# Two-layer transformer with mixtures of experts: GpSimd's gather and scatter programs unrolled, and layer 0's result rows written to a place of their own instead of being added up in DRAM

## The chip, the cores and the metric

One NeuronCore of one Trainium2 chip runs the whole program in one launch. The metric is the device time of an execution in microseconds (us).

## The reference

Two layers over x of 2 batches x 512 tokens x 256 channels (T = 1024 tokens in all), all in float32. Each layer is an adaLN block: a modulated layer norm, causal attention with 16 heads, a gated residual, a second modulated norm, and a mixture of experts.

```
x = x + ga * attention(layernorm(x) * (1 + ca) + sa)
h = layernorm(x) * (1 + cb) + sb
x = x + gb * mixture(h)
layer 0: 8 experts, top 2:  y = sum over the 2 chosen e of gate[e] * (W2[e] silu(W1[e] h + b1[e]) + b2[e])
layer 1: 16 experts, top 4: h + sum over the 4 chosen e of gate[e] * (W2[e] act(W1[e] rms(h) + b1[e]) + b2[e])
```

What matters here is the sum over a token's chosen experts. In layer 0 each token has exactly two result rows of 256 floats, in layer 1 four.

## The kernel before, in words

**The mixture.** Tokens are sorted by expert into tiles of 128 places. Every tile belongs to one expert: layer 0 has 23 tiles (SLOTS_T[0]), layer 1 has 47. Places that no token takes are filled with pad rows T to T + 127, one for each partition (lane). DVE works out a place for each token and choice, PE turns that into a table by matmuls with zeros and ones (L1520, into bank 4), and DVE makes two tables of it: `weight` (gate of the row at place p of tile i) and `token` (its row number in DRAM, L1171 to L1174). `te` holds each tile's expert (L1175 to L1178).

**One tile** then runs through the engines. POOL gathers its 128 rows from DRAM (`xs`, which the trace calls token_rows) into one of four buffers `xt` with an indirect DMA (L612). PE transposes it (L1534), multiplies by W1 (L1549 bias, L1552), transposes (L1561) and multiplies by W2 (L1570 bias, L1573), each for another tile of a pipeline four steps deep. ACT applies the gate weight and writes the result tile to one of four buffers `yt` (L820, semaphore y_sb). POOL adds its 128 rows into DRAM with an indirect DMA that adds (L619), into one of two tables of sums, by the parity of the tile. ACT may write `yt` of tile i only when the add of tile i - 4 has landed.

**POOL's program** is the order in question. POOL is a queue that runs in order. In step s it waits for its index copy, for the result of tile s - 7 (LAG = 7), for the landing of the add of tile s - 9, and for PE's transposes of tile s - 3; then it copies the indices of step s + 1 out of the table `token` into a small tile `indices` (`pick`, L603), gathers tile s, and adds tile s - 7. So two adds are in flight at most. Eleven steps are written out, the middle of each layer is a loop of four steps a turn, and the last seven steps, which have only an add, are written out too. A layer has SLOTS_T + 7 steps.

**After the last tile** SP (in order as well) waits for the adds of tiles of one parity, issues four loads of that table (256 KB each, L508), waits for the other parity and issues four more. For each quarter of the tokens, DVE (POOL for the last quarter) adds the two tables, multiplies by the gate and adds to x (L1257 to L1261; POOL L660 to L667). In layer 0 the norm and attention of layer 1 follow behind it; in layer 1 the output's stores (L516). Meanwhile PE and DVE work out layer 1's modulation (PE after the last y_sb of layer 0, L1280 and L1299; DVE up to L893).

**Zeroing.** The four tables of sums (two a layer, 1152 KB each) are zeroed by SP's DMAs (L468) during layer 0's attention, behind the loads of the expert weights (L464) and the small transfers of maxima (L442).

Of the kernel before, what the change touches and what calls it, by code (L numbers as in the profile page):

```python
# [10 lines left out]
P = 128  # L11
D = 256
# [3 lines left out]
T = B * S  # L16
NT = T // P
# [26 lines left out]
TOPK = [2, 4]  # L44
# [10 lines left out]
UNROLL = 4  # L55
STEADY = 7
LAG = 7
PICKS_BEFORE = [0, SLOTS_T[0] + LAG]
POOL_STEADY = 11
# [7 lines left out]
def build_kernel(nc, dram, out):  # L67
    with ExitStack() as ctx:
        def sb(name, shape, dt=F32):
            return ctx.enter_context(nc.sbuf_tensor(name, shape, dt))  # L70

        def sem(name):
            return ctx.enter_context(nc.semaphore(name))
# [153 lines left out]


        xs = [nc.dram_tensor(f"token_rows{l}", [T + P, D], F32, kind="Internal") for l in range(2)]
        acc = [[nc.dram_tensor(f"sums{l}_{a}", [T + P, D], F32, kind="Internal") for a in range(2)] for l in range(2)]  # L230


        ld_const = sem("ld_const")
# [66 lines left out]
        token_picked = sem("token_picked")  # L300
        placed_ps = sem("placed_ps")
        acc_loaded = sems("acc_loaded", 4)
        h_rows = sem("h_rows")
# [118 lines left out]
        def _(sp):  # L422
# [20 lines left out]
                        qr[SROWS + r:SROWS + r + 1, (g // 2) % 2, hl:hl + HG, :],  # L443
                        mT[r * 16:(r + 1) * 16, g % 2, :]).then_inc(m_rows[l][g % 2], 16)

            ZERO_AT = [0, 1, 5, 6]

            for l in range(2):
                spread_unit(sp, nc.sync, l, 0, (0, 1), spread[0])
# [7 lines left out]
                for g in range(NG):  # L457
                    if g in (3, 5):

                        u = (g + 1) // 2  # L460
                        spread_unit(sp, nc.sync, l, u, (1,), spread[u])
                    send_maxima(l, g)
                    piece = slice(g * WROW[l], (g + 1) * WROW[l])
                    nc.sync.dma_start(big[:, piece], dram[f"moe{l}"][:, piece]).then_inc(ld_w_lo[l], 16)  # L464
                    if l == 0 and g in ZERO_AT:

                        z = ZERO_AT.index(g)
                        nc.sync.dma_start(acc[z // 2][z % 2][:, :].rearrange("(t p) c -> p t c", p=P),  # L468
                                          zeros[:, :].unsqueeze(1).broadcast_to([P, NT + 1, D])).then_inc(zeroed, 16)
# [31 lines left out]


                sp.wait_ge(y_ps[l], n)
                for a in ((n - 2) % 2, (n - 1) % 2):
                    for r in (a, a + 2):
                        sp.wait_ge(y_summed[r], TILES_BEFORE[l + 1][r])
                    for m in (3, 0, 1, 2):
                        nc.sync.dma_start(acc_in[:, a, 2 * m:2 * m + 2, :],  # L508
                                          acc[l][a][2 * m * P:(2 * m + 2) * P, :].rearrange("(t p) c -> p t c", p=P)
                                          ).then_inc(acc_loaded[m], 16)  # L510
            for m in (0, 3, 1, 2):
                if m < NT // 2 - 1:
                    sp.wait_ge(x_new[1], m + 1)
# [8 lines left out]
        def _(pool):  # L522
# [10 lines left out]
            for l in range(2):  # L533
# [58 lines left out]
                def pick(ii, off):  # L592

                    i, r, _ = tile_at(ii, off)
                    n = SLOTS_T[l]
                    gathers, adds = takes_part(ii, off)
                    if gathers and adds:
                        src, dst = token[:, bass.ds(i - LAG, LAG + 1)][:, ::LAG], indices[:, r, :]
                    elif gathers:
                        src, dst = token[:, i:i + 1], indices[:, r, 1:2]  # L600
                    else:
                        src, dst = token[:, i - LAG:i - LAG + 1], indices[:, r, 0:1]
                    nc.gpsimd.tensor_copy(dst, src).then_inc(token_picked, 1)  # L603

                def takes_part(ii, off):

                    known, n = isinstance(ii, int), SLOTS_T[l]
                    return not known or off < n, not known or 0 <= off - LAG < n

                def gather(off):  # L610
                    r = off % 4
                    nc.gpsimd.indirect_dma_start(  # L612
                        out=xt[:, r, :], out_offset=None, in_=xs[l][:, :],
                        in_offset=bass.IndirectOffsetOnAxis(ap=indices[:, r, 1:2], axis=0)).then_inc(xt_loaded[r], 16)

                def add_rows(off):
                    r = off % 4
                    place_r = (off + LAG) % 4
                    nc.gpsimd.indirect_dma_start(  # L619
                        out=acc[l][off % 2][:, :],  # L620
                        out_offset=bass.IndirectOffsetOnAxis(ap=indices[:, place_r, 0:1], axis=0),
                        in_=yt[:, r, :], in_offset=None, compute_op=ALU.add).then_inc(y_summed[r], 16)

                def pool_step(ii, off):
                    gathers, adds = takes_part(ii, off)
                    i, _, _ = tile_at(ii, off)

                    pool.wait_ge(token_picked, PICKS_BEFORE[l] + i + 1)
                    if adds:

                        pool.wait_ge(y_sb[l], i - LAG + 1)
                        if not (isinstance(i, int) and i < LAG + 2):
                            _, r2, rnd2 = tile_at(ii, off - LAG - 2)
                            pool.wait_ge(y_summed[r2], TILES_BEFORE[l][r2] + 16 * rnd2 + 16)
                    if gathers and not (isinstance(i, int) and i < 3):

                        pool.wait_ge(xT_ps[l], i - 2)
                    if not isinstance(ii, int) or off + 1 < SLOTS_T[l] + LAG:
                        pick(ii, off + 1)
                    if gathers:  # L640
                        gather(off)
                    if adds:
                        add_rows(off - LAG)

                pool.wait_ge(zeroed, 16 * 6)
                pool.wait_ge(rows_stored[l], 16 * B)
                pool.wait_ge(tokens_ready, l + 1)
                pick(0, 0)
                for s in range(POOL_STEADY):
                    pool_step(0, s)  # L650
                with pool.Fori(0, (SLOTS_T[l] - POOL_STEADY) // UNROLL) as ii:
                    for q in range(UNROLL):
                        pool_step(ii, POOL_STEADY + q)
                for s in range(SLOTS_T[l], SLOTS_T[l] + LAG):
                    pool_step(0, s)

                m = NT // 2 - 1
                rng = slice(2 * m, 2 * m + 2)
# [186 lines left out]
        def _(dve):  # L845
# [74 lines left out]
            for l in range(2):  # L920
# [157 lines left out]
                E, K = EXPERTS[l], TOPK[l]  # L1078
                if l == 0:
                    dve.wait_ge(ld_small, 64)  # L1080
                oh = onehot[:, 0:NT * K * E].rearrange("p (t k e) -> p t k e", t=NT, k=K)
                ch = chosen[:, 0:NT * E].rearrange("p (t e) -> p t e", t=NT)
                for b in range(B):
# [49 lines left out]
                for b in range(B):  # L1133
# [16 lines left out]
                    for t in range(b * TB, (b + 1) * TB):  # L1150
                        c = slice(t * K, (t + 1) * K)
                        nc.vector.tensor_tensor(
                            in_tile(l, t), first[:, c].unsqueeze(2).broadcast_to([P, K, MT[l]]),
                            iota_t128[:, 0:MT[l]].unsqueeze(1).broadcast_to([P, K, MT[l]]),
                            ALU.is_equal).then_inc(tile_of[l], 1)
                        nc.vector.tensor_tensor(
                            at_p[:, c, :], place[:, c].unsqueeze(2).broadcast_to([P, K, P]),
                            iota_p.unsqueeze(1).broadcast_to([P, K, P]), ALU.is_equal)
                        dve.wait_ge(tile_of[l], t + 1)
                        nc.vector.tensor_scalar(weighed_tile(l)[:, c, 0, :], in_tile(l, t), left[:, t:t + 1], None,  # L1160
                                                ALU.mult).then_inc(place_of[l], 1)
# [7 lines left out]
                sums = ps[4][:, 0:2 * MT[l]].rearrange("p (a c) -> p a c", a=2)  # L1169
                w = slice(0, MT[l])  # L1170
                count(nc.vector.tensor_copy(weight[:, w], sums[:, 1, :]))  # L1171
                link(nc.vector.tensor_scalar(token_f[:, w], sums[:, 0, :], 0.0, lane[:, 0:1], ALU.is_equal, ALU.mult))
                link(nc.vector.tensor_tensor(token_f[:, w], token_f[:, w], sums[:, 0, :], ALU.subtract))
                nc.vector.tensor_scalar(token[:, w], token_f[:, w], float(T), None, ALU.add).then_inc(tokens_ready, 1)  # L1174
# [523 lines left out]
```

## Time and profile before

| | |
|---|---|
| median of 3 runs | 691.54 us (691.23 to 694.9) |
| span of the profiled execution, first to last instruction | 693.0 us |
| layer 0's mixture, first gather to last add landed | 203.8 to 287.6 us |
| layer 1's mixture, first gather to last add landed | 502.6 to 676.6 us |
| busy share over the span: PE, DVE, ACT, POOL | 77%, 54%, 35%, 39% |
| indirect DMAs on POOL | 70 gathers, 70 adds |
| mean granted TensorE clock | 0.881 of full speed |

The profile covers one execution; its span is the time that it shows for itself, and it lies 1.5 us above the median. An indirect DMA has two durations: how long the instruction holds POOL, and the time from its start to the landing of its data, which is when its semaphore is complete. "issue" is time in which the engine waited for nothing that the profile shows.

### The profile page before, as it was taken

How to read it: one execution, taken by the hardware profiler on the slowest of the kernel's cores; microseconds unless marked ns; L12 is line 12 of the kernel's file. 1: busy time of each engine (PE TensorE's matmuls, PEld its weight loads, DVE VectorE, ACT ScalarE, POOL GpSimd, SP SyncE). 2: the span in 40 equal slices, each digit the busy share in tenths (PEclk: the TensorE clock that was granted, in tenths of full speed). 3: DMA queues.
4: the chain of work that ended last, by engine and by line, in shares of the span. 5: the costliest groups of instructions: out<-in, count | busy, mean ns of one | idle time of the engine just before them, and what ended most of it. 6: DMA issues, size and time to landing. Idle time of an engine off the chain costs nothing.

```text
span 693.0 us, 10488 instructions
## 1 busy us (share of the span) xinstructions
PE 531.5 (77%) x3140; PEld 343.4 (50%) x3141; DVE 371.5 (54%) x854; ACT 245.4 (35%) x542; POOL 269.0 (39%) x285
## 2 busy tenths in 40 slices
PE   4679977987649777637897879863679999999960
PEld 3344544545547665315454445543636666666630
DVE  4855756545663222288386636566934444544424
ACT  1225534554132222003264335521424444444420
POOL 2300103001026888430001150046048888888852
PEclk9898989899658999959799989995679999999995
DMA  7097466634103545707828272173013444444445
GB/s 269 2 131 145 122 100 110 127 106 178 61 16 67 83 80 70 156 2 96 99 81 136 62 124 94 50 318 111 0 54 70 77 79 73 79 79 83 71 52 180
DMA packets 44499, 67.41 MB, mean 97 GB/s; under 512 B 6417, under 2 KB 37857, under 8 KB 44209
## 3 DMA queue, kind: packets, MB, share of 16 engines
q1 hardware_dynamic: 29872, 45.45, 27.4%
q0 software_dynamic: 14592, 21.51, 19.4%
q8 instruction: 21, 0.34, 0.2%
q14 instruction: 14, 0.11, 0.1%
HBM read 36.83 MB, written 17.30 MB: 78 GB/s over the span
## 4 chain that ended last, share of the span: by engine, by line
PE 51%; DMA 15%; DVE 13%; ACT 6%; POOL 5%; issue 5%; SPq 4%; POOLq 0%; DVEq 0%; ACTq 0%
PE bank L1552 13%; PE bank L1573 6%; DMA big<-parts 5%; DMA sums<-ptm,indices 5%; PE bank L1399 5%; PE bank L1442 4%; PE bank L1418 4%; ACT ptm L757 3%; SPq L409 3%; PE bank L1372 3%; DVE mx L1022 3%; PE bank L1520 3%; DMA big<-mT 2%; PE bank L1534 2%; POOL ptm L612 2%
## 5 line engine op out<-in xcount | busy, mean ns | idle before, releaser
L1022 DVE TENSOR_REDUCE mx<-bank 128x4 f32<-128x512 f32 (+2 forms) x96 | 99.2, 1042 | 76.1 <-PE bank L1402 75.4
L619 POOL DMA_INDIRECT sums<-ptm,indices x70 | 113.2, 1617 | 22.9 <-issue 21.2
L1552 PE MATMUL bank<-big,ptm 128*128 x280 | 111.7, 522 | 0.0
L757 ACT ACTIVATE ptm<-bank 128x512 f32<-128x512 f32 x160 | 90.3, 596 | 53.3 <-PE bank L1421 51.0
L1418 PE MATMUL bank<-big 98*128 98x128 bf16 (+3 forms) x256 | 68.8, 326 | 22.8 <-DMA big<-mT 14.2
L1399 PE MATMUL bank<-big 96*128 96x128 bf16 (+3 forms) x256 | 67.3, 329 | 15.8 <-DMA big<-parts 11.6
L409 POOL DMA_DIRECT2D big<-parts x24 | 13.0, 553 | 166.1 <-PE bank L1421 166.1
L612 POOL DMA_INDIRECT ptm<-token_rows,indices x70 | 70.3, 1004 | 17.0 <-issue 12.9
L1573 PE MATMUL bank<-big,ptm 128*128 (+1 forms) x280 | 72.1, 379 | 0.0
L603 POOL COPY indices<-token 128x2 uint32 (+2 forms) x84 | 43.4, 516 | 57.1 <-DVE token L1174 42.6
L1214 DVE TENSOR_SCALAR tok<-bank 128x256 f32<-128x256 f32 x47 | 19.9, 424 | 84.9 <-PE bank L1552 84.9
L1552 PEld LDWEIGHTS bank<-big,ptm 128*128 128x128 f32 x280 | 51.0, 197 | 26.6 <-issue 23.6
L531 POOL TENSOR_TENSOR rstd<-vareps,neghalf 128x4 f32<-128x4 f32 x8 | 8.6, 1072 | 122.6 <-DVE vareps L906 122.6
L1418 PEld LDWEIGHTS bank<-big 98*128 98x128 bf16 x256 | 26.6, 104 | 54.6 <-ACT ptm L757 25.2
L1402 PE MATMUL bank<-constb 128*128 128x128 bf16 x256 | 52.7, 234 | 0.0
L1421 PE MATMUL bank<-constb 128*128 128x128 bf16 x256 | 50.9, 233 | 0.0
L804 ACT ACTIVATE ctxden<-tok 128x256 f32<-128x256 f32 x47 | 19.6, 417 | 86.2 <-DVE tok L1214 86.2
L1573 PEld LDWEIGHTS bank<-big,ptm 128*128 128x128 f32 (+1 forms) x280 | 47.5, 190 | 4.8
L1399 PEld LDWEIGHTS bank<-big 96*128 96x128 bf16 x256 | 26.6, 104 | 36.1 <-issue 25.1
L820 ACT ACTIVATE ptm<-bank,weight 128x256 f32<-128x256 f32 x70 | 33.1, 473 | 27.9 <-PE bank L1573 25.5
L1442 PE MATMUL bank<-ptm,big 128*32 128x128 f32 (+3 forms) x512 | 39.4, 447 | 1.4 <-ACT ptm L757 1.4
L1534 PE MATMUL bank<-consts,ptm 128*128 128x128 f32 x140 | 28.6, 288 | 11.2 <-DMA ptm<-token_rows,indices 11.2
(174 smaller groups left out, 872.3 us busy)
## 6 DMA issues: line engine op xcount, KB each, us to landing
big<-parts SPq DMA_DIRECT2D x72, 128.0 KB, 7.7
big<-in_moe_dram SPq DMA_DIRECT2D x8, 768.0 KB, 4.3
big<-in_moe_dram SPq DMA_DIRECT2D x1, 6144.0 KB, 19.6
sums<-zeros SPq DMA_DIRECT2D x4, 1152.0 KB, 6.4
ptm<-sums SPq DMA_DIRECT2D x16, 256.0 KB, 4.6
big<-in_moe_dram SPq DMA_DIRECT2D x8, 432.0 KB, 4.0
big<-parts POOLq DMA_DIRECT2D x24, 128.0 KB, 5.1
wqkv<-in_wqkv_dram SPq DMA_DIRECT2D x2, 768.0 KB, 6.8
```

What stands on the lines that cost most here:

```text
L603: nc.gpsimd.tensor_copy(dst, src).then_inc(token_picked, 1)
L612: nc.gpsimd.indirect_dma_start(out=xt[:, r, :], out_offset=None, in_=xs[l][:, :], in_offset=bass.IndirectOffsetOnAxis(ap=indices[:, r, 1:2 ...
L619: nc.gpsimd.indirect_dma_start(out=acc[l][off % 2][:, :], out_offset=bass.IndirectOffsetOnAxis(ap=indices[:, place_r, 0:1], axis=0), in_=y ...
L757: nc.scalar.activation(dst, src, ACT.Exp).then_inc(b_exp[l], 1)
L1022: nc.vector.tensor_reduce(mx[:, g % 2, :].rearrange("p (j i) -> p j i", j=HG)[:, j0:j0 + n, i], a_view(c), AX.X, ALU.max).then_inc(a_max[l ...
L1399: nc.tensor.matmul(dst[:, j, :], qr[0:SROWS, u % 2, hl, i * P:(i + 1) * P], kr[0:SROWS, u % 2, hl, 0:w], start=True, stop=False)
L1402: last = nc.tensor.matmul(dst[:, j, w - P:w], ident_b, causal_b, start=False, stop=True)
L1418: nc.tensor.matmul(ps[4 + c % 2][:, col:col + S - k * P], kr[0:MROWS, u % 2, hl, k * P:(k + 1) * P], qr[0:MROWS, u % 2, hl, k * P:S], star ...
L1421: last = nc.tensor.matmul(ps[4 + c % 2][:, col:col + P], causal_b, ident_b, start=False, stop=True)
L1442: last = nc.tensor.matmul(ps[6][32 * j:32 * j + 32, k * P:S], vaug[:, b * TB + k, hg * HG + j, :], pt[:, g % 2, j, PK[k]:PK[k] + S - k * P ...
L1552: last = nc.tensor.matmul(dst, xtT[:, off % 2, k, :], moe_w1(l, k, e), start=False, stop=(k == KD - 1))
L1573: last = nc.tensor.matmul(dst, hidT[0:HK[l], off % 2, k, :], moe_w2(l, k, e), start=False, stop=(k == 1))
```

## The change

- `pick` and the tile `indices` are gone. Gathers and scatters read their indices straight from a column of a table. Both layers' steps are written out: no loop, 30 steps in layer 0 and 54 in layer 1.
- Each gather now waits only for PE's transposes of tile i - 4. The wait for a result stands directly before the scatter.
- Layer 0: the table `pairs` has two halves of T + 128 rows, one for each choice. A second table of indices, `dest`, names the half, and `put_rows` writes the rows without addition. It waits for the landing of the scatter before it (i - 1), where the add waited for i - 2. SP waits for all scatters before it loads anything.
- Layer 1: `add_rows` adds as before, with the wait for i - 2, into the two tables that were zeroed for it. Two of the four zeroings are gone.
- DVE carries the choice through the table of places: the token's number has 2048 added for choice 1 (`leftk`), which is taken off again afterwards.

```diff
-        indices = sb("indices", [P, 4, 2], U32)
+        dest = sb("dest", [P, MT[0]], U32)
+        upper = sb("upper", [P, MT[0]])
+        leftk = sb("leftk", [P, NT * TOPK[0]])
...
+        pairs = nc.dram_tensor("pairs", [2 * ROWS, D], F32, kind="Internal")
+        sums = [nc.dram_tensor(f"sums{a}", [ROWS, D], F32, kind="Internal") for a in range(2)]
...
-            ZERO_AT = [0, 1, 5, 6]
+            ZERO_AT = [0, 1]
...
                 sp.wait_ge(y_ps[l], n)
+                if l == 0:
+                    for r in range(4):
+                        sp.wait_ge(y_summed[r], TILES_BEFORE[1][r])
                 for a in ((n - 2) % 2, (n - 1) % 2):
-                    for r in (a, a + 2):
-                        sp.wait_ge(y_summed[r], TILES_BEFORE[l + 1][r])
+                    if l == 1:
+                        for r in (a, a + 2):
+                            sp.wait_ge(y_summed[r], TILES_BEFORE[2][r])
...
+                def gather(i):
+                    if i >= 4:
+                        pool.wait_ge(xT_ps[l], i - 3)
                     nc.gpsimd.indirect_dma_start(
+                        out=xt[:, i % 4, :], out_offset=None, in_=xs[l][:, :],
+                        in_offset=bass.IndirectOffsetOnAxis(ap=token[:, i:i + 1], axis=0)).then_inc(xt_loaded[i % 4], 16)
+                def put_rows(i):
+                    pool.wait_ge(y_sb[0], i + 1)
+                    if i >= 1:
+                        pool.wait_ge(y_summed[(i - 1) % 4], 16 * ((i - 1) // 4) + 16)
                     nc.gpsimd.indirect_dma_start(
+                        out=pairs[:, :], out_offset=bass.IndirectOffsetOnAxis(ap=dest[:, i:i + 1], axis=0),
+                        in_=yt[:, i % 4, :], in_offset=None).then_inc(y_summed[i % 4], 16)
+                def add_rows(i):
+                    pool.wait_ge(y_sb[1], i + 1)
+                    if i >= 2:
+                        pool.wait_ge(y_summed[(i - 2) % 4], TILES_BEFORE[1][(i - 2) % 4] + 16 * ((i - 2) // 4) + 16)
...
+                for s in range(SLOTS_T[l] + LAG):
+                    if s < SLOTS_T[l]:
+                        gather(s)
+                    if s >= LAG:
+                        if l == 0:
+                            put_rows(s - LAG)
+                        else:
+                            add_rows(s - LAG)
...
+                if l == 0:
+                    link(nc.vector.tensor_scalar(upper[:, :], placed[:, 0, :], SECOND - 0.5, float(SECOND), ALU.is_gt, ALU.mult))
+                    link(nc.vector.tensor_tensor(upper[:, :], placed[:, 0, :], upper[:, :], ALU.subtract))
+                    link(nc.vector.tensor_scalar(token_f[:, w], upper[:, :], 0.0, lane[:, 0:1], ALU.is_equal, ALU.mult))
+                    link(nc.vector.tensor_tensor(token_f[:, w], token_f[:, w], upper[:, :], ALU.subtract))
+                    count(nc.vector.tensor_scalar(token[:, w], token_f[:, w], float(T), None, ALU.add))
+                    link(nc.vector.tensor_scalar(upper[:, :], placed[:, 0, :], SECOND - 0.5, float(ROWS), ALU.is_gt, ALU.mult))
+                    nc.vector.scalar_tensor_tensor(dest[:, :], token_f[:, w], float(T), upper[:, :], ALU.add,
+                                                   ALU.add).then_inc(tokens_ready, 1)
```

In `link` DVE waits for its own instruction before the next; in `count` it doesn't.

## Rows read from the trace of the kernel before

**Rows 1.** The page: chain that ended last by engine, and the group of picks.

```profile
PE 51%; DMA 15%; DVE 13%; ACT 6%; POOL 5%; issue 5%; SPq 4%; POOLq 0%; DVEq 0%; ACTq 0%
...
L603 POOL COPY indices<-token 128x2 uint32 (+2 forms) x84 | 43.4, 516 | 57.1 <-DVE token L1174 42.6
```

**Rows 2.** Windows: us; busy (x) of PE, PEld, DVE, ACT, POOL; PEclk; DMA share; GB/s.

```profile
225.55:268.07 42.52, 31.93 (x187) 25.39 (x185) 11.41 (x27) 10.75 (x27) 36.43 (x40) 1.00 0.50 81
...
560.00:600.00 40.00, 40.00 (x169) 25.52 (x168) 19.13 (x48) 17.29 (x48) 32.98 (x37) 1.00 0.47 75
```

**Rows 3.** Timeline of POOL, layer 0, one steady step (start us, us, instruction).

```profile
241.91 1.59 POOL L619 DMA_INDIRECT sums<-ptm,indices  x1 [0.30 <-issue]
242.93 0.77 POOL L603 COPY indices<-token 128x2 uint32 x1
243.87 1.00 POOL L612 DMA_INDIRECT ptm<-token_rows,indices  x1 [0.16 <-POOL indices L603]
245.18 1.60 POOL L619 DMA_INDIRECT sums<-ptm,indices  x1 [0.30 <-issue]
```

**Rows 4.** Timeline of ACT, layer 0: the first two result tiles.

```profile
216.41 0.47 ACT L820 ACTIVATE ptm<-bank,weight 128x256 f32<-128x256 f32 x1 [0.88 <-PE bank L1573]
...
218.55 0.47 ACT L820 ACTIVATE ptm<-bank,weight 128x256 f32<-128x256 f32 x1 [0.88 <-PE bank L1573]
```

**Rows 5.** Timeline of POOL, layer 0: adds of tiles 0, 15 and 22.

```profile
218.94 1.64 POOL L619 DMA_INDIRECT sums<-ptm,indices  x1 [0.30 <-PE bank L1534]
...
268.07 1.59 POOL L619 DMA_INDIRECT sums<-ptm,indices  x1 [0.30 <-issue]
...
283.77 1.55 POOL L619 DMA_INDIRECT sums<-ptm,indices  x1 [0.41 <-issue]
```

**Rows 6.** Chain in order of time, the end of layer 0's mixture (start us, us, what).

```profile
283.77 3.88 DMA sums<-ptm,indices
287.71 0.37 SPq L508
288.12 5.92 DMA ptm<-sums
```

**Rows 7.** Chain in order of time, layer 1's last adds, tiles 44 and 46.

```profile
666.27 0.48 ACT ptm L820
...
667.52 3.91 DMA sums<-ptm,indices
...
671.50 0.69 issue
672.19 4.44 DMA sums<-ptm,indices
```

**Rows 8.** Source view of L619, the adds (durations ns min/median/max, then landings).

```profile
L619 POOL DMA_INDIRECT sums<-ptm,indices x70: 1552/1597/1829, 218.9 to 672.2; - x70
...
DMA to landing us min/median/max: 3.6/3.8/4.4
```

**Rows 9.** Source view of L612, the gathers.

```profile
L612 POOL DMA_INDIRECT ptm<-token_rows,indices x70: 967/1007/1117, 203.8 to 652.1; - x70
...
DMA to landing us min/median/max: 2.6/2.8/4.6
```

**Rows 10.** Timelines of DVE and POOL: layer 0's token table and first gather.

```profile
202.41 0.18 DVE L1173 TENSOR_TENSOR token_f<-token_f,bank 128x24 f32<-128x24 f32 x1
202.62 0.18 DVE L1174 TENSOR_SCALAR token<-token_f 128x24 uint32<-128x24 f32 x1
...
203.78 1.12 POOL L612 DMA_INDIRECT ptm<-token_rows,indices  x1 [0.38 <-issue]
```

**Rows 11.** Timeline of SP: the eight loads of layer 0's sums.

```profile
285.58 4.08 SPq L508 DMA_DIRECT2D ptm<-sums  x8
```

**Rows 12.** Timeline of DVE: the end of layer 1's modulation.

```profile
290.12 0.41 DVE L893 TENSOR_SCALAR modbc<-bank 128x256 f32<-128x256 f32 x1
```

**Rows 13.** Waits between 118 and 150 us, where the dropped zeroings run.

```profile
PE bank L1418 <- DMA big<-mT: 2.9, 1, 2.9
```

More of the change, by code:

```diff
@@ L229, in build_kernel, with summand @@
         xs = [nc.dram_tensor(f"token_rows{l}", [T + P, D], F32, kind="Internal") for l in range(2)]
-        acc = [[nc.dram_tensor(f"sums{l}_{a}", [T + P, D], F32, kind="Internal") for a in range(2)] for l in range(2)]
+        pairs = nc.dram_tensor("pairs", [2 * ROWS, D], F32, kind="Internal")
+        sums = [nc.dram_tensor(f"sums{a}", [ROWS, D], F32, kind="Internal") for a in range(2)]
+        def summand(l, a, lo, hi):
+            src = pairs[a * ROWS + lo:a * ROWS + hi, :] if l == 0 else sums[a][lo:hi, :]
+            return src.rearrange("(t p) c -> p t c", p=P)
         ld_const = sem("ld_const")
@@ L590, in _ @@
                         nc.gpsimd.tensor_tensor(x[:, rng, :], x[:, rng, :], tok[:, rng, :], ALU.add).then_inc(h_added, 1)
[L592 to L611, printed above, removed]
-                    nc.gpsimd.indirect_dma_start(
-                        out=xt[:, r, :], out_offset=None, in_=xs[l][:, :],
-                        in_offset=bass.IndirectOffsetOnAxis(ap=indices[:, r, 1:2], axis=0)).then_inc(xt_loaded[r], 16)
@@ L616, in add_rows @@
-                def add_rows(off):
-                    r = off % 4
-                    place_r = (off + LAG) % 4
-                    nc.gpsimd.indirect_dma_start(
[L620 to L643, printed above, removed]
@@ new lines, in add_rows @@
+                def add_rows(i):
+                    pool.wait_ge(y_sb[1], i + 1)
+                    if i >= 2:
+                        pool.wait_ge(y_summed[(i - 2) % 4], TILES_BEFORE[1][(i - 2) % 4] + 16 * ((i - 2) // 4) + 16)
+                    nc.gpsimd.indirect_dma_start(
+                        out=sums[i % 2][:, :], out_offset=bass.IndirectOffsetOnAxis(ap=token[:, i:i + 1], axis=0),
+                        in_=yt[:, i % 4, :], in_offset=None, compute_op=ALU.add).then_inc(y_summed[i % 4], 16)
@@ L646, in _ @@
+                pool.wait_ge(zeroed, 16 * 4)
                 pool.wait_ge(rows_stored[l], 16 * B)
                 pool.wait_ge(tokens_ready, l + 1)
[L648 to L655, printed above, removed]
+                for s in range(SLOTS_T[l] + LAG):
[6 more added lines that the diff above has]
+                            add_rows(s - LAG)
@@ L1080, in _ @@
                     dve.wait_ge(ld_small, 64)
+                    dve.wait_ge(ld_const, 16)
+                    by_k = leftk[:, :].rearrange("p (t k) -> p t k", k=K)
+                    count(nc.vector.tensor_copy(by_k[:, :, 0], left))
+                    count(nc.vector.tensor_scalar(by_k[:, :, 1], left, float(SECOND), None, ALU.add))
                 oh = onehot[:, 0:NT * K * E].rearrange("p (t k e) -> p t k e", t=NT, k=K)
@@ L1159, in _ @@
                         dve.wait_ge(tile_of[l], t + 1)
-                        nc.vector.tensor_scalar(weighed_tile(l)[:, c, 0, :], in_tile(l, t), left[:, t:t + 1], None,
-                                                ALU.mult).then_inc(place_of[l], 1)
+                        if l == 0:
+                            nc.vector.tensor_tensor(weighed_tile(0)[:, c, 0, :], in_tile(0, t),
+                                                    leftk[:, c].unsqueeze(2).broadcast_to([P, K, MT[0]]),
+                                                    ALU.mult).then_inc(place_of[0], 1)
+                        else:
+                            nc.vector.tensor_scalar(weighed_tile(1)[:, c, 0, :], in_tile(1, t), left[:, t:t + 1], None,
+                                                    ALU.mult).then_inc(place_of[1], 1)
                 pk = picked[0:1, 0:n * E].rearrange("p (t e) -> p t e", t=n)
@@ L1168, in _ @@
                 dve.wait_ge(placed_ps, l + 1)
-                sums = ps[4][:, 0:2 * MT[l]].rearrange("p (a c) -> p a c", a=2)
+                placed = ps[4][:, 0:2 * MT[l]].rearrange("p (a c) -> p a c", a=2)
                 w = slice(0, MT[l])
[L1171 to L1174, printed above, removed]
+                count(nc.vector.tensor_copy(weight[:, w], placed[:, 1, :]))
+                if l == 0:
+                    link(nc.vector.tensor_scalar(upper[:, :], placed[:, 0, :], SECOND - 0.5, float(SECOND), ALU.is_gt, ALU.mult))
[6 more added lines that the diff above has]
+                                                   ALU.add).then_inc(tokens_ready, 1)
+                else:
+                    link(nc.vector.tensor_scalar(token_f[:, w], placed[:, 0, :], 0.0, lane[:, 0:1], ALU.is_equal, ALU.mult))
+                    link(nc.vector.tensor_tensor(token_f[:, w], token_f[:, w], placed[:, 0, :], ALU.subtract))
+                    nc.vector.tensor_scalar(token[:, w], token_f[:, w], float(T), None, ALU.add).then_inc(tokens_ready, 1)
                 link(nc.vector.tensor_reduce(tef[:, 0:n], pk, AX.X, ALU.add))
```

11 lines of the change are left out of this document (4 added, 7 removed).

## The prediction, made before the change was run

> **What bounds the kernel now.** I read the page first. Its chain is half PE, and POOL has only 5% of it, though the picks alone keep POOL busy for 43.4 us [rows 1]. So what a shorter program on POOL is worth must be read stage by stage, and the table of windows does that. In layer 1's mixture PE is busy 40.00 of 40 us and POOL 32.98: PE sets the pace. In layer 0's mixture PE is busy 31.93 of 42.52 us and POOL 36.43, the rest of POOL's time being short gaps of issue [rows 2]. POOL sets the pace there. Its timeline shows why: from one add to the next are 3.27 us (241.91 to 245.18), made of the add's 1.60, what is left of the pick, a gather of 1.00 and gaps of 0.16 and 0.30 [rows 3]. ACT's first two result tiles came 2.14 us apart, before any add was issued [rows 4]; that is how fast the other engines can go.
>
> At layer 0's end the gathers are over and each add waits for the landing of the one two before it. Tile 15's add starts at 268.07 and tile 22's at 283.77, so 2.24 us each, with two in flight [rows 5]. The last lands 3.88 us after its start, at 287.65. Then come SP's loads and DVE [rows 6].
>
> **What the change does, part by part.**
>
> *The wait of the plain scatter.* This is the term that decides. Put i waits until put i - 1 has landed, not i - 2. So each of layer 0's 22 steps between puts costs at least the landing time L, plus the restart of a waiting POOL. The restart stands at the end of layer 1: tile 44's add lands at 671.43, tile 46's, which waited for it with no pick between, starts at 672.19, so 0.76 us [rows 7]. The same step without any wait would be gather, put and two gaps: 1.00 + 1.00 + 0.60 = 2.60 us if a put holds POOL as long as a gather. The gather between two puts lies inside the wait for the landing and costs nothing; if landings became that short, it would set the pace of 2.60.
>
> *L itself* is in no row, for no plain scatter runs before. An add holds POOL 1.60 us and lands 3.8 us after its start [rows 8]. A gather, also 128 rows of 1 KB without addition, holds it 1.00 and lands after 2.8, at least 2.6 [rows 9]. I bound L by 2.6 and 3.8 and take 2.8: the put has the gather's bytes, rows and indices and lacks the addition, which needs the old row read before the new one is written. The step is then 2.8 + 0.76 = 3.56 us, longer than the 3.27 it replaces and much longer than the 2.24 of the tail.
>
> The Trainium skill (DMA: Bandwidth & Descriptors, Anatomy of one DMA — SWDGE path) says otherwise of the direction: most of the fixed cost of a small transfer is the receipt of the last write, and DRAM (HBM) is the slowest target. [...] What a slow write would do is the first rival.
>
> *Head of layer 0.* DVE's table chain has four more dependent instructions ahead of the token signal. One costs 0.21 us (202.41 to 202.62) [rows 10]: +0.8. Between the end of the token table (202.80) and the first gather (203.78) lie 0.98 us with two picks; a restart without a pick is 0.76: -0.2. Together +0.6 for the first gather, +0.5 for the first results, since later picks are gone too. The first y ended at 216.88 [rows 4] and now ends at 217.4. Before, the first add stood behind gather 7, which itself waited for that y; now gather 7 goes ahead of the wait, and put 0 starts at 217.4 + 0.76 = 218.15 (before 218.94 [rows 5]). The broadcast multiply of DVE in place of the scalar one has as many elements, and the two `leftk` instructions run while DVE waits for PE's gate logits: nothing; uncovered, they would cost 0.4.
>
> *Sum to the last landing.* Put 22 starts at 218.15 + 22 x 3.56 = 296.5 and lands at 299.3. Before it was 287.65: **+11.6 us**. PE and ACT wait for free `yt` buffers meanwhile, at no further cost, because their own pace is 2.14.
>
> *SP's loads.* Before, the four loads of the first parity were issued from 285.58, two us ahead of the last landing [rows 11], and the load that DVE waited for was issued 0.47 us after that landing and took 5.92 [rows 6]. Now all eight come after it, the deciding one is the sixth, and one issue takes 0.5 us: it leaves at about +2.5. **+2.0 us.** Layer 1's modulation, done at 290.53 before the loads landed at 294.04 [rows 6, 12], hangs on the last y, which needs put 18 landed (about 285 us) and so ends near 297, with the loads landing near 307: hidden. If put 18 were later still, both move together.
>
> *Layer 1.* First gathers earlier by the picks and the shorter restart: -0.3. Steady tiles: PE's, unchanged. Tail: tile 44's add started 0.77 us after its y was done, pick included [rows 7], and the restart without one is 0.76: nothing. Code written out in place of the loop: POOL has no loop cost in its steady step [rows 3] beyond the gaps; nothing, and if instruction fetches stalled it, layer 1's cover is POOL's idle 7 of 40 us [rows 2] and layer 0's is the wait.
>
> *Two zeroings less.* In their stretch the only wait for a transfer is PE's 2.9 us for the maxima, which come from SP's queue ahead of the zeroing [rows 13]: nothing, at most -0.5.
>
> **Sum**: 11.6 + 2.0 - 0.3 = +13.3 us. Against the profiled span that is 706.3; that execution lies 1.5 above the median, so the forecast is 691.5 + 13.3 = **704.8 us**. Each 0.1 us of L moves it by 23 x 0.1 = 2.3. With L from 2.6 to 3.0 it is 700.2 to 709.4, the forecast's own range.
>
> **The rivals.**
>
> 1. *Writes to DRAM are confirmed more slowly than reads from it.* After its 1.60 on POOL the add still took 2.2 us, the gather 1.8 [rows 8, 9]. If that 0.4 belongs to the write and not to the addition, L = 1.0 + 2.2 = 3.2: put 22 lands at 218.15 + 22 x 3.96 + 3.2 = 308.5, +20.8, in all +22.5: **714 us**. For it: the add's row; against: the addition also reads the old rows. This is also the direction of the Trainium skill's rule.
> 2. *The long hold of POOL is the scatter's, not the addition's.* Then a put holds 1.60, L is 3.4 (gather's 1.8 behind it) to 3.8: **718.6 to 727.8 us**. For it: every scatter in the trace holds 1.55 or more; against: the one difference known between the two forms is the addition's extra read.
> 3. *The other side: plain rows land so soon that the wait is over before the gather between is issued.* Then POOL's own 2.60 sets the pace and L is at most 2.3: put 22 lands at 218.15 + 57.2 + 2.3 = 277.7, -10.0; with the loads -8.3: **683.3 us**. It decides from 22 steps + L = 67.8 us on; with the full restart that is L = 2.2. Against: the quickest of 70 gathers took 2.6. For: a restart might overlap the gather's own issue, which with L = 2.6 and the steady step's 0.30 gap in place of 0.76 gives 22 x 2.9 + 2.6 = 66.4, 1.4 less, so about 690.
> 4. *Nothing to see*: the slower steps and the saved picks cancel. That takes L of 2.2 to 2.4 or such an overlap: **688 to 695 us**.
>
> **How the numbers follow.** Forecast 0.47, rival 1 0.20, rival 2 0.18, rival 3 0.09, rival 4 0.06. The range reaches from 697, where a restart shorter by a few tenths would put the forecast, to 721, which holds rival 1 and the lower half of rival 2; outside lie rivals 3 and 4 and rival 2's end, some 0.2. A measurement of this kernel tells about 0.5% or 3.5 us from no change. Faster by more: 0.08 (rival 3); within: 0.07; slower: 0.85.
>
> **What the changed profile would show.** The step: POOL's timeline with puts about 3.5 us apart and idle time before each, released by the DMA of the put before; PE waiting for ACT or for gathers, its busy share in that stretch down from 0.75 to about 0.7. L: the put's landing in its source view, near 2.8, and its duration near 1.0. The tail: no speeding up after the last gather. The loads: eight in one run after the last landing. Layer 1: the same 40 of 40 us on PE and the last adds at the same distance from the last y. I am wrong if puts stand 2.6 to 3.2 us apart, if they land in under 2.4, or if layer 1's tiles change their pace.

## The result and the profile after

The changed kernel is slower: 698.68 us median of 5 runs (697.45 to 702.78) against 692.52 us, a ratio of 1.0098 (95% interval 1.0063 to 1.0134). That is inside the range on record (697 to 721), near its lower end, and on the side it named, but about half of the +13.3 us that was forecast, and below the forecast's own range (700.2 to 709.4). Ratios are of executions in the fast state; one of the twelve of after_again below took 1765 us and is left out of its ratio.

The profiled execution spans 700.9 us. POOL's timeline in layer 0, two steady steps and the tail (start us, us, instruction, idle before it), answers to [rows 3] and [rows 5]:

```profile
225.64 0.99 POOL L615 DMA_INDIRECT pairs<-ptm,dest  x1 [0.97 <-ACT ptm L803]
226.93 0.97 POOL L606 DMA_INDIRECT ptm<-token_rows,token  x1 [0.30 <-issue]
228.83 0.99 POOL L615 DMA_INDIRECT pairs<-ptm,dest  x1 [0.93 <-DMA pairs<-ptm,dest]
...
267.31 0.99 POOL L615 DMA_INDIRECT pairs<-ptm,dest  x1 [0.94 <-DMA pairs<-ptm,dest]
270.50 0.99 POOL L615 DMA_INDIRECT pairs<-ptm,dest  x1 [2.20 <-DMA pairs<-ptm,dest]
...
289.48 0.97 POOL L615 DMA_INDIRECT pairs<-ptm,dest  x1 [2.20 <-DMA pairs<-ptm,dest]
```

A put holds POOL 0.99 us, then comes the gather, which ends at 227.90. The put before has landed 2.43 us after its start, at 228.07, and the next put starts 0.76 us later: of POOL's 0.93 us of idle time 0.17 are the rest of the landing and 0.76 the restart. From put to put are 3.19 us, and that does not change when the gathers end (267.31 to 270.50): only the idle time grows. The first row names ACT as what ended the wait, since a put waits for its result too. But that result had been ready since 223.14, 2.5 us before. From put 1 on, all results were ready 1.4 to 9.7 us ahead of their puts, and each put started 0.7 to 0.8 us after the landing of the one before. Before the change a step was 3.27 us [rows 3], but 2.24 in the tail [rows 5].

The source views of the puts (L615) and gathers (L606), against [rows 8, 9]:

```profile
L615 POOL DMA_INDIRECT pairs<-ptm,dest x23: 969/987/999, 219.2 to 289.5; - x23
...
DMA to landing us min/median/max: 2.4/2.4/2.5
```

```profile
L606 POOL DMA_INDIRECT ptm<-token_rows,token x70: 940/992/1102, 205.8 to 657.7; - x70
...
DMA to landing us min/median/max: 2.6/2.8/3.3
```

The chain at layer 0's end, against [rows 6]. Two of the steps between puts and the end:

```profile
286.31 2.43 DMA pairs<-ptm,dest
...
288.77 0.70 issue
289.48 2.42 DMA pairs<-ptm,dest
...
294.50 5.47 DMA ptm<-pairs
```

The step is 2.43 for the landing and 0.74 for the restart. The load that DVE waits for is the sixth, issued at 294.50, 2.6 us after the last landing. The last put lands at 291.90; DVE's first combination starts at 299.99, 8.09 us later, where it was 6.42 before (294.07 - 287.65).

Layer 1 is as it was: in the windows view PE is busy 40.00 of 40 us from 560 to 600, while POOL's share fell with the picks (32.98 before [rows 2]).

```profile
560.00:600.00 40.00, 40.00 (x169) 25.37 (x167) 19.24 (x48) 17.53 (x48) 30.79 (x25) 1.00 0.49 79
```

From its first gather to the start of its last add layer 1 takes 168.60 us (511.55 to 680.15), before 169.55 (502.64 to 672.19).

**Where the 6 us are.** From layer 0's first gather to its last landing 86.07 us (205.83 to 291.90) against 83.87: +2.2. From there to DVE +1.7. DVE's longer chain for the tables +0.6 (from its copy of the weights to the first gather 2.38 us against 1.74). Layer 1's mixture -0.95. That makes +3.6.

The two profiled spans differ by more, 7.9 us (700.9 against 693.0). The other 4.4 us lie in stretches whose work is the same in both kernels: 1.4 ahead of layer 0's tables, and 3.0 between DVE's first combination and layer 1's first gather (211.56 us against 208.57). The first are TensorE's clock. In the windows view the first fence is before and has PE alone (us, busy, PEclk, DMA share, GB/s); the second is after and has PE, PEld, DVE, ACT and POOL ahead of PEclk:

```profile
166.00:170.00 4.00, 2.47 (x33) 1.00 0.78 332
```

```profile
166.00:170.00 4.00, 3.30 (x29) 1.16 (x22) 0.21 (x1) 0.60 (x1) 0.73 (x1) 0.62 0.77 326
```

The granted clock was 0.62 of full speed on the mean of these 4 us, that is, partly at the lower of its two levels (1.2 GHz), although the work is the same in both kernels. In both, PE had been idle for 0.69 us, waiting for ACT's exponentials, just before the group of 32 matmuls at 165 us; that group took 4.05 us after and 2.36 before. This fall is in 4 of the 14 profiled executions of this document, so it comes and goes. The 3.0 us come and go as well: in a second execution of the changed kernel that stretch took 207.66 us.

### The profile page after: what moved, and what is told of

Its sections match the earlier page's. It is cut to its first block, busy times and chain, and to the rows that moved or that the text cites. A ratio compares the mean times of both kernels' runs of the same rounds, so it can differ in the third digit from the quotient of the medians.

```text
span 700.9 us, 10178 instructions
## 1 busy us (share of the span) xinstructions
PE 536.8 (77%) x3140; PEld 346.7 (49%) x3141; DVE 372.6 (53%) x860; ACT 245.7 (35%) x542; POOL 235.0 (34%) x201
## 3 DMA queue, kind: packets, MB, share of 16 engines
q0 software_dynamic: 12384, 21.51, 16.4%
## 4 chain that ended last, share of the span: by engine, by line
PE 53%; DMA 17%; DVE 13%; ACT 6%; issue 5%; SPq 4%; POOL 1%; POOLq 0%; DVEq 0%; ACTq 0%
PE bank L1555 13%; PE bank L1576 7%; DMA pairs<-ptm,dest 6%; DMA big<-parts 5%; PE bank L1402 5%; PE bank L1445 5%; PE bank L1421 4%; ACT ptm L740 3%; SPq L416 3%; PE bank L1375 3%; DVE mx L1005 2%; PE bank L1537 2%; DMA big<-mT 2%; PE bank L1552 2%; PE bank L1564 2%
## 5 line engine op out<-in xcount | busy, mean ns | idle before, releaser
L606 POOL DMA_INDIRECT ptm<-token_rows,token x70 | 68.8, 983 | 70.0 <-DVE dest L1172 24.9
L624 POOL DMA_INDIRECT sums<-ptm,token x47 | 74.5, 1584 | 31.9 <-ACT ptm L803 30.2
L1445 PE MATMUL bank<-ptm,big 128*32 128x128 f32 (+3 forms) x512 | 42.9, 479 | 1.4 <-ACT ptm L740 1.4
L1316 PE MATMUL bank<-consts,tok 128*128 128x128 f32 x80 | 14.3, 337 | 30.9 <-DVE tok L898 26.5
```

The lines of the kernel that those rows point to most:

```text
L606: nc.gpsimd.indirect_dma_start(out=xt[:, i % 4, :], out_offset=None, in_=xs[l][:, :], in_offset=bass.IndirectOffsetOnAxis(ap=token[:, i:i ...
L624: nc.gpsimd.indirect_dma_start(out=sums[i % 2][:, :], out_offset=bass.IndirectOffsetOnAxis(ap=token[:, i:i + 1], axis=0), in_=yt[:, i % 4, ...
L1445: last = nc.tensor.matmul(ps[6][32 * j:32 * j + 32, k * P:S], vaug[:, b * TB + k, hg * HG + j, :], pt[:, g % 2, j, PK[k]:PK[k] + S - k * P ...
```

## The experiments

### The program written out, nothing else

Layer 0 adds as before the change, with the wait for the add two before; only `pick`, `indices` and the loops are gone.

```diff
-                pick(0, 0)
-                for s in range(POOL_STEADY):
-                    pool_step(0, s)
...
+                for s in range(SLOTS_T[l] + LAG):
+                    if s < SLOTS_T[l]:
+                        gather(s)
+                    if s >= LAG:
+                        add_rows(s - LAG)
```

> The kernel before with POOL's program written out and indices read from the token table; layer 0 still adds, with the wait for the add two before. Theory (the loss is the serial wait for each put's landing, and writing the program out helps a little): layer 0's steady step is 1.60 + 0.30 + 1.00 + 0.30 = 3.20 us instead of 3.27, the first add starts 1 to 2 us earlier, the tail keeps its pairs of about 4.6 us, layer 1 keeps PE's pace: 2 to 3 us faster than before, about 690. Rival (writing the program out is itself what costs, by instruction fetches or because gathers run further ahead): slower than before by several us, about 697.

Measured: 688.77 us, ratio to before 0.9917 (0.9885 to 0.995). POOL's timeline, the first add and two steady ones:

```profile
217.32 1.63 POOL L605 DMA_INDIRECT sums<-ptm,token  x1 [1.58 <-ACT ptm L781]
...
242.87 1.59 POOL L605 DMA_INDIRECT sums<-ptm,token  x1 [0.30 <-ACT ptm L781]
244.77 0.99 POOL L596 DMA_INDIRECT ptm<-token_rows,token  x1 [0.30 <-issue]
246.06 1.59 POOL L605 DMA_INDIRECT sums<-ptm,token  x1 [0.30 <-issue]
```

The step is the 3.19 us expected. The first add comes 13.04 us after the first gather at 204.28 (before 15.16), and from first gather to last landing (284.29) are 80.0 us, before 83.9. So this half of the change gains 0.8% alone, more than my 2 to 3 us; the end of the interval nearest to no change is 3.5 us. The rival, that unrolling costs, is out.

### The same with the old waits

Every step waits first for all that it waited for before, and then gathers and adds.

```diff
+                    if s >= LAG:
+                        pool.wait_ge(y_sb[l], s - LAG + 1)
+                    if s >= LAG + 2:
+                        pool.wait_ge(y_summed[(s - LAG - 2) % 4], TILES_BEFORE[l][(s - LAG - 2) % 4] + 16 * ((s - LAG - 2) // 4) + 16)
+                    if 3 <= s < SLOTS_T[l]:
+                        pool.wait_ge(xT_ps[l], s - 2)
```

> As unroll_only, but each step first waits for everything that the step waited for before (the result, the add two before, the transposes of tile s - 3), and only then gathers and adds. Unroll_only took 3.9 us off the stretch from layer 0's first gather to its last landing (80.0 against 83.9), 2.1 of it before the first add. Theory (a gather that no longer stands behind the wait for a result lets the first add start sooner): first gather to first add goes back from 13.0 to about 15 us, the steady step stays at 3.19, the stretch is about 82.1. Rival (it was the missing picks): the first add stays at 13.0 to 13.5 and the stretch at 80.

One execution, 692.21 us. First gather to first add: 14.43 us (204.60 to 219.03), between 13.04 and 15.16 and nearer the theory. The last add starts 77.8 us after the first gather (at 282.41), in the kernel without the old waits 76.5, before 80.0. One execution of each is thin, for the same POOL program brings its first put 12.77 to 13.69 us after the first gather in four executions (below). What separates the causes better is the distance from ACT's first result to the first add: 0.28 us without the old waits, 1.72 with them, 2.06 before. So 1.4 us of the earlier start come from gathers that no longer stand behind a result; the rest, 0.4 us ahead of that result and 0.3 behind it, went with the picks and the loop.

### Puts that add

The changed kernel with the addition put back into its puts, and nothing else in POOL's program but its wait for two more zeroings, since both halves of the table have to be zeroed first.

```diff
-                        in_=yt[:, i % 4, :], in_offset=None).then_inc(y_summed[i % 4], 16)
+                        in_=yt[:, i % 4, :], in_offset=None, compute_op=ALU.add).then_inc(y_summed[i % 4], 16)
```

> The changed kernel, but layer 0's put adds to its row again (both halves of the table zeroed first); the wait for the put just before stays. Theory: a step is landing plus restart, so 3.8 + 0.76 = 4.56 us instead of 3.19; 22 steps and the last landing cost 31 us more than the changed kernel: about 730. Rival (POOL's own work sets the step, the wait is hidden): 1.60 + 1.00 + 0.60 = 3.20, no change against the changed kernel: about 699.

Measured: 730.25 us, ratio 1.0514 (1.0462 to 1.0566). The chain in layer 0:

```profile
273.15 3.78 DMA pairs<-ptm,dest
...
276.98 0.73 issue
277.70 3.77 DMA pairs<-ptm,dest
```

3.78 for the landing and 0.77 for the restart make the step of 4.55 us. The same wait therefore costs what the landing costs, and the time went where landing plus restart said (730) and not to POOL's own work (699). The puts hold POOL 1.586 us here and 0.987 in the changed kernel, and land after 3.8 and 2.4: both differences belong to the addition.

### Pads apart

In the changed kernel every tile's pads go to the same 128 rows, and successive tiles may both write them; therefore the wait for the put just before. Nothing reads those rows: SP's loads take rows 0 to T - 1 of each half. Here four successive tiles have pad rows of their own, and that wait is loosened to the put two before, or dropped.

```diff
+            for r, off in enumerate((0, ROWS, 2 * ROWS - T, 2 * ROWS + P - T)):
+                nc.gpsimd.memset(padoff[:, r:r + 1], float(off))
...
+                    padadd = token_f[:, MT[0]:2 * MT[0]]
+                    count(nc.vector.scalar_tensor_tensor(padadd.rearrange("p (a b) -> p a b", b=4),
+                                                         placed[:, 0, :].rearrange("p (a b) -> p a b", b=4), 0.0,
+                                                         padoff[:, :].unsqueeze(1).broadcast_to([P, MT[0] // 4, 4]),
+                                                         ALU.is_equal, ALU.mult))
...
+                    link(nc.vector.tensor_tensor(upper[:, :], upper[:, :], padadd, ALU.add))
...
-                    if i >= 1:
-                        pool.wait_ge(y_summed[(i - 1) % 4], 16 * ((i - 1) // 4) + 16)
```

> The changed kernel, with the pad rows of four successive tiles sent to four places of their own (two more DVE instructions on the way to the token signal), so that a put need only wait for the landing of the put two before. Theory: layer 0's step falls to POOL's own 1.00 + 0.30 + 1.00 + 0.30 = 2.60 us, and after the last gather the puts follow the results at 1.6 to 2.2 us: the last put lands about 20 us earlier, 678 to 682 us. Rival (the loss is in the eight loads that now wait for the last put, and in layer 1): at most 2 us off the changed kernel, 697 to 699.

> As pads_apart_wait2, with no wait for a landing at all on POOL; only ACT's wait for the buffer of four tiles before is left. Theory: with two in flight the wait is over already, so the same time as with it within 1 us, 678 to 682. A second theory, that landings limit the rate even with two in flight, gives 2 us or more less than pads_apart_wait2. The rival of the loads gives 697 to 699.

Measured: 681.26 us with the wait for i - 2 (ratio 0.9813, 0.9773 to 0.9852) and 681.44 us without (0.9805, 0.9773 to 0.9838). POOL's timeline without the wait:

```profile
240.34 0.99 POOL L616 DMA_INDIRECT pairs<-ptm,dest  x1 [0.30 <-issue]
241.64 0.97 POOL L609 DMA_INDIRECT ptm<-token_rows,token  x1 [0.31 <-PE bank L1544]
242.91 0.99 POOL L616 DMA_INDIRECT pairs<-ptm,dest  x1 [0.30 <-issue]
...
270.27 0.96 POOL L616 DMA_INDIRECT pairs<-ptm,dest  x1 [0.62 <-ACT ptm L804]
```

The step is 2.57 us, POOL's own work, and the last put starts 65.5 us after the first gather at 204.81, in the changed kernel 83.65. Taking the wait off turns the change from 1.0% slower into 1.9% faster than before, although the edit adds two instructions to DVE's chain. That settles the cause: the wait for the put just before, and not the unrolling, the scatter or layer 1. That the two forms are equal also says that two puts in flight are enough, and it rules out the second theory, that landings limit the rate. No run drops the wait while the pads stay together.

Not all 18 us reach DVE's first combination: it starts 14.26 us after the start of the last put, in the changed kernel 10.51. Two lines of DVE's timeline of the same run show what is late next, layer 1's modulation (L877), which holds DVE until 284.4 while POOL already had its loads at 280.76:

```profile
283.96 0.41 DVE L877 TENSOR_SCALAR modbc<-bank 128x256 f32<-128x256 f32 x1
284.53 0.85 DVE L1267 TENSOR_TENSOR ptm<-ptm 128x512 f32<-128x512 f32 x1 [0.16 <-DVE modbc L877]
```

### Loads in pairs

The changed kernel, whose eight loads now all follow the last put, with both halves of a quarter one behind the other.

```diff
+                if l == 0:
+                    for m in (3, 0, 1, 2):
+                        for a in range(2):
+                            nc.sync.dma_start(acc_in[:, a, 2 * m:2 * m + 2, :],
+                                              summand(0, a, 2 * m * P, (2 * m + 2) * P)).then_inc(acc_loaded[m], 16)
```

> The changed kernel, with layer 0's eight loads in the order that DVE uses them: both halves of a quarter behind each other. In the changed kernel 8.1 us lie between the last landing and DVE's first combination, before the change 6.4. Theory (the wait is SP's issue of six loads at 0.5 us and then the transfer): the deciding load becomes the fourth, about 7.1 us. Rival (the transfer's bandwidth alone sets it): 8.1, since POOL's quarter goes first either way and the same bytes are under way. In all at most 1 us off the changed kernel.

> The changed kernel once more, unaltered, on the same chip as loads_paired_timed. Its first profile lost 1.5 us to a fall of TensorE's granted clock near 166 us that the profile of before does not have, and more such in layer 1's attention. Theory (such falls come and go from run to run): the median stays at 1 per cent over before, about 699; the last landing comes 86.1 us after the first gather, as in the first profile. Rival (the falls belong to the changed kernel, for instance through the two zeroings less): the fall near 166 us is there again.

> The kernel of loads_paired, timed. In its one look DVE's first combination came 7.0 us after the last landing instead of 8.1, and the first combination took 2.7 us instead of 4.5, because POOL's own was further ahead. Theory (both gains are real and lie on the way): 3 us under the changed kernel, about 696. Rival (only the order of issue counts, the rest of the 4 us by which that one execution was quicker was the clock): 1 us under it, about 698.

Measured: 694.74 us in one profiled execution; timed in twelve, 695.85 us (ratio to before 1.0024, 0.9997 to 1.0052), beside 698.69 us of the changed kernel on the same chip (1.0093, 1.0059 to 1.0128). In the profiled execution the last put lands at 289.84 and DVE starts at 296.84, so 7.0 us instead of 8.1: the order of the loads counts, and the rival, that only the bytes do, is out. DVE's timeline there, and that of the changed kernel:

```profile
296.84 1.17 DVE L1264 TENSOR_TENSOR ptm<-ptm 128x512 f32<-128x512 f32 x1 [5.29 <-DMA ptm<-pairs]
298.05 0.69 DVE L1266 TENSOR_TENSOR ptm<-ptm,modbc 128x512 f32<-128x512 f32 x1
```

```profile
299.99 1.17 DVE L1260 TENSOR_TENSOR ptm<-ptm 128x512 f32<-128x512 f32 x1 [6.54 <-DMA ptm<-pairs]
301.19 1.64 DVE L1262 TENSOR_TENSOR ptm<-ptm,modbc 128x512 f32<-128x512 f32 x1
```

The same multiplication takes DVE 1.64 us while POOL runs its own over another quarter, and 0.69 us after POOL is done. POOL's own takes 1.59 us beside DVE's and 1.26 alone. The pair order starts POOL's quarter earlier and so gives back 1.1 us of waiting and 1.9 of slowed work (first combination 2.66 us instead of 4.54). These 3 us fit the timed medians, which are 2.8 apart; by the ratios it is 0.7% or 4.8 us. The changed kernel with this order alone can't be told from the kernel before.

The second execution of the unaltered changed kernel had no fall of the clock near 166 us: PEclk 1.00 in that window.

```profile
166.00:170.00 4.00, 2.48 (x35) 1.00 0.63 264
```

From first gather to last landing it took 86.4 us (203.67 to 290.11), as the first profile's 86.1.

### The best kernel, and what binds behind the wait

Pads apart without the wait, loads in pairs, and the signal to POOL as soon as `token` is there.

> pads_apart_no_wait, the loads in pairs, and the token signal sent to POOL as soon as the token table is there, with the second index table after it. In pads_apart_no_wait DVE is busy with layer 1's modulation until 284.4, 3.6 us after the loads were there for POOL, so the paired loads bring nothing here; the earlier token signal starts layer 0 about 1.2 us sooner and the modulation moves with it. Theory (after the wait is gone the modulation sets layer 0's end): 680 us, 1 us under pads_apart_no_wait. Rival (the loads set it): 2 us or more under it.

> As best, with DVE's work on the rows of layer 1's modulation moved behind the first combination and norm of layer 0's end. Theory (in best this work, waiting for PE's 10 us of modulation matmuls, holds DVE back while the loads have landed): the first combination starts 3 to 4 us earlier, about 677 us. Rival (PE's modulation matmuls hold the next projection back anyway, so DVE's order is worth nothing): as best.

Measured: best 677.95 us (0.9769, 0.9724 to 0.9813), best_order 681.39 us (0.9825, 0.979 to 0.9861). Best is 2.5 us under pads_apart_no_wait by the ratios, nearer the rival's 2 us than the theory's 1, though the two intervals overlap. What the theory said of the order is so: DVE's first combination follows its last instruction on the modulation directly.

```profile
284.42 0.69 DVE L1274 TENSOR_TENSOR ptm<-ptm 128x512 f32<-128x512 f32 x1 [0.16 <-DVE modbc L884]
```

It starts 12.39 us after the start of the last put, where it was 14.26. The earlier token signal brings the first gather 0.6 us closer to DVE's tables (2.07 against 2.68 us behind the copy of the weights), half of the 1.2 expected. No gain is shown further on: the first put comes 13.95 us after the first gather, in pads_apart_no_wait 12.39, and one and the same kernel differs by 0.8 us there (loads_paired 13.55, loads_paired_timed 12.77).

In best_order DVE's first combination did start 4.1 us sooner, and the time did not follow; that theory fell. The rival's time, as best, can't be excluded, for the intervals overlap; its reason is not what the trace shows, as ACT's first query projection waits for DVE and not for TensorE (the row below). Two more runs are best again and a kernel that differs from best by these lines:

```diff
+                    if l == 1 and n == 1:
+                        modulation_rows(1, 0)
...
-                    modulation_rows(1, 0)
```

> The kernel of best once more, beside best_late_rows on the same chip: 2.3 per cent under before, 676 to 679.

> As best, with DVE's work on the rows of layer 1's modulation still later than in best_order: behind both norms and the first two splits of layer 1's projections. In best_order the first combination came 4.1 us earlier than in best, but the second batch's norm stood behind the moved work and the start of layer 1's query projections (ACT at 300.8 against 300.5) did not move. Theory (what binds there is the second norm, so work moved behind it frees both): ACT's first query projection at about 297 and the time 3 us under best. Rival (TensorE's modulation and projections bind, or the moved work now delays the splits by its own 4 us): as best or slower.

Measured: 679.02 us (0.9773, 0.9742 to 0.9803) and 676.45 us (0.9747, 0.9717 to 0.9777). ACT's first query projection of layer 1 in best_order and in best_late_rows:

```profile
300.78 0.69 ACT L710 ACTIVATE tok<-bank,qkb 128x512 f32<-128x512 f32 x1 [7.84 <-DVE qkb L915]
```

```profile
296.36 0.69 ACT L710 ACTIVATE tok<-bank,qkb 128x512 f32<-128x512 f32 x1 [4.22 <-DVE qkb L915]
```

It waits for DVE's L915, which stands behind the second batch's norm. Moving the modulation behind the first norm only shifted it ahead of the second. Moved behind both, it starts 25.75 us after the start of the last put, in best_again 28.47: 2.7 us are freed. The median is 2.6 us lower than best's on the same chip, though the two intervals overlap. This version is 2.5% faster than the kernel before.

## Why the prediction came out as it did

The side and the mechanism were right; one term of the sum was mis-sized, and the range held at its low end. That is in part luck: 697 had been set for a shorter restart, and what came was a shorter landing. By its own signs the prediction was off, too: it called itself wrong if puts stood 2.6 to 3.2 us apart, and they stood 3.19 apart.

1. **The bound of before**, POOL in layer 0 and PE in layer 1: right. Unrolling moved layer 0, and layer 1's PE stayed at 40 of 40 us.
2. **The wait as the deciding term, landing plus restart**: right, and shown by dose. The step was 3.19 us at a landing of 2.43, 4.55 at 3.78, and POOL's own 2.57 without the wait (forecast 2.60).
3. **L = 2.8 by the gather: the term that was mis-sized.** It measured 2.43, below my lower bound of 2.6. "L from 2.6" took the quickest gather as a floor for a write, and no row supported that. 22 steps x 0.37 (3.56 - 3.19) and 0.4 in the last landing are 8.5 us of the sum. The hold of 1.00 for the put was right (0.99), and so was the restart behind a landing (0.74 to 0.77). But the same 0.76 was also set for put 0, which waits for ACT's result and not for a landing: it started 0.29 us after that result, in both executions of the changed kernel.
4. **Rival 1**, slow confirmation of writes, is refuted: after its 0.99 on POOL the put takes 1.4 us, the gather 1.8, the add 2.2. The put's data take the least, so the add's 2.2 belong to the addition. The Trainium skill (DMA: Bandwidth & Descriptors, Anatomy of one DMA — SWDGE path) has the fit 2.0 us plus bytes / 436 GB/s, the making of the descriptors included; that is an estimated 2.3 us for 128 KB from start to landing. The put's 2.43 agrees with it; the gather's 2.8 and the add's 3.8 lie above. Its remark that DRAM is the heaviest target for the receipt does not show here: the put, which writes to DRAM, lands sooner than the gather, which reads from it.
5. **Rival 2**, the hold of 1.60 as the scatter's own, is refuted by the put's 0.99 and by the puts that add, which hold POOL 1.59.
6. **Last landing**: forecast 299.3, measured 291.90, or 290.11 in the second execution. With the measured step and landing and that execution's first put at 217.36 (forecast 218.15) the sum gives 217.36 + 22 x 3.19 + 2.43 = 290.0.
7. **Loads, +2.0**: measured +1.7. That DVE's work beside POOL's takes more than twice as long was not seen, though it stood in the trace of before too.
8. **Layer 1, -0.3**: measured -0.95. It is not the puts: unroll_only has the same 168.56 us from first gather to last add. **Head, +0.6**: the first gather came 0.64 us later behind DVE's copy of the weights, and the first put 13.3 to 13.7 us after the first gather, forecast 13.8.
9. **"Both move together"**, of the modulation and the loads: in the changed kernel the modulation was done 6.5 us before the loads, hidden as forecast; with the wait gone it was late, and that took best_late_rows to mend.
10. **PE's busy share** in layer 0's steady steps was to fall from 0.75 to about 0.7. It rose to 0.84 (39.42 of 47 us from 220 to 267); why is open.
11. The forecast of +13.3 comes down to 4.8 with L alone put right; the terms read from the traces make +3.6, and the paired runs +4.1 to +8.9 (1.0059 to 1.0128). The 3 us between the middle of that and the traces stay open. The stretches outside these terms differ by more than that between two executions of the same kernel (211.56 and 207.66 us in layer 1's attention), so one profiled execution of each can't say where they are. The profiled execution of before is no middle one either: it took 694.9 us, the only one of its three times above the span of 693.0, and so lay 3.4 above the median and not 1.5.

## What to carry to other kernels

A wait for the landing of the transfer just before turns a queue's throughput into landing plus restart. Price it with both, and look at the stretch where transfers used to overlap: there (the tail, 2.24 to 3.19 us) it cost most, while the steady steps even gained. Before accepting such a wait, ask which rows really collide; by the program here only the pads do, which nothing reads, and giving them places of their own turned a loss of 1% into a gain of 2%. Once a long wait is gone, look again at what it had covered.

## What the runs showed of the hardware that was not expected

- A scatter of 128 rows of 1 KB into DRAM without addition lands 2.4 us after its start, sooner than the gather of as many rows (2.8). With addition it takes 3.8, and holds POOL 1.59 us instead of 0.99.
- The restart of a waiting POOL depends on whom it waits for: a put starts 0.7 to 0.8 us after the landing of a DMA, but 0.29 us after ACT's result (first puts of both executions of the changed kernel).
- By the queue lines of the profile's page the software queue's packets fell from 14592 to 12384 with the 23 plain puts, so by 96 each, at the same 21.51 MB, and were 14592 again when the puts added:

```profile
q0 software_dynamic: 12384, 21.51, 16.4%
```

- DVE and POOL running elementwise work on SBUF side by side: DVE's 128x512 multiplication 1.64 us instead of 0.69, POOL's 1.59 instead of 1.26.
